# Graph attention and a two-expert layer on one core: a longer lead of blocks, routing and tables in parts, and a new order of products at each tile's start

## The chip, the cores and the metric

The kernel runs on one core of one Trainium2 chip, in one launch. The metric is the device time of that core in microseconds (us). Below, TensorE is the matmul engine, VectorE, ScalarE, GpSimd and SyncE the four others; SyncE issues most transfers.

## The reference, cut to what matters

Everything is float32. N = 4096 nodes, D = 512, E = 8 experts.

```python
q = layernorm(x) @ Wq.T + bq;  k = key @ Wk.T + bk;  v = value @ Wv.T + bv
s = (q @ k.T) / 4096 ** 0.5 * adj
s = where(abs(s) < 1e-5, -1e9, s)
x1 = x + (softmax(s) @ v) @ Wm.T + bm
g = softmax(layernorm(x1) @ Wg + bg);  the two largest of 8, renormalised to sum 1
out = x1 + sum over the two chosen e of gate_e * (layernorm(x1) @ We[e].T + be[e])
```

## The kernel before, in words

Each float32 operand is held as a high and a low half in float16, and a product is three float16 matmuls (high by high, high by low, low by high). A group of products over the 512 of the contraction, 12 matmuls of 128x512, is called a block of TensorE work here.

The first stage folds the weights (Wq with Wk, Wv with Wm), projects the values and writes the queries of all 32 tiles of 128 rows to DRAM. The keys stay in `kT`, the values in `v`.

The second stage, `attend(t)`, runs over the tiles t. A tile's 4096 scores are 8 pieces c of 512 columns. `scores(t, c)` is a block into one of four PSUM banks; VectorE adds a bias and multiplies by the adjacency (`times_adj`), ScalarE takes the absolute value (`absolute`), VectorE masks and takes the maximum (`mask`). When all 8 pieces are there, ScalarE takes exponentials (`exponent`, two passes a piece), VectorE makes the low half (`low_half`), and SyncE has the piece transposed by a DMA. `times_values(t, c)` is again a block; all 8 of a tile add up in one PSUM bank, `o_bank`. Because the exponentials need the whole row, the value products of tile t-1 are spread over the iteration of tile t, and those of its pieces 6 and 7 fall into the iteration of tile t+1. There `residual(t-2)` on VectorE reads `o_bank` (x1_done) before `times_values(t-1, 0)` may write it.

Every engine follows an order that is written out by hand, and all are in order. On VectorE the order at a tile's start is: low halves 0 to 2 of the old tile, `times_adj` 0, low half 3, `mask` 0, `times_adj` 1, low half 4, `mask` 1, low halves 5 and 6, `times_adj` 2, low half 7, `mask` 2, `residual(t-2)`. On ScalarE it is: exponents 0 to 3, `absolute` 0, exponent 4, `absolute` 1, exponents 5, 6 and 7, `absolute` 2. The queries of the next tile are fetched from DRAM when the last scores of this one are done.

After each tile the rows are routed: layer norm, `gate_logits` on TensorE, `route_top2` and `route_gates` on VectorE, `ranks` on TensorE, `route_slots` on VectorE; GpSimd then scatters the normed rows to slots in DRAM, region by region for each expert (`scatter_row`). The tokens are in two halves, each with its own table of 39 blocks of 128 slots. `tables(h)` on VectorE computes it in 19 dependent steps: after tile 17 for half 0, within the last stage for half 1.

The third stage runs 78 blocks: SyncE loads the block's 128 rows, TensorE turns them (`turn_block`) and multiplies with the expert's weights (`multiply_block`), VectorE adds the bias (`block_bias`), ScalarE multiplies with the gate (`block_gate`), GpSimd adds the rows to the output in DRAM by an indirect DMA (`add_block`). An add waits for the four-back one, and at the first block of an expert's run for the ones before it in its half. The first LEAD blocks are all of half 0, the last LEAD of half 1, and the middle ones alternate between the halves. The experts' weights, split into halves during the second stage and kept in DRAM, are loaded over `kT` by `load_expert` on ScalarE's queue.

Of the kernel before, what the change touches and what calls it, by code (L numbers as in the profile page):

```python
# [19 lines left out]
def graph_attention_moe_kernel(nc, x, adj, keyT, valueT, Wq, bq, Wk, bk, Wv, bv, WmT, bm, Wg, bg, WeT, be, outs):  # L20
# [37 lines left out]
    LEAD = 15  # L58
# [22 lines left out]
    with ctx:  # L81
# [173 lines left out]
        we_dram = nc.dram_tensor("we_halves", (2 * E, P, 2, 2 * D), F16, kind="Internal").ap()  # L255
# [154 lines left out]
        def _(sp):  # L410
# [101 lines left out]
            def pad_first_regions():  # L512

                sp.wait_ge(tables_done, 1)
                for e in range(E):
                    at = sp.value_load(pad_at[0:1, 0, e:e + 1], min_val=0, max_val=(DUMMY - 1) * P)
                    sp.dma_start(slots[0][bass.ds(at, P), :], pad_row[:, :]).then_inc(padded[0], 16)
# [9 lines left out]
            pad_first_regions()  # L527
# [43 lines left out]
            expert_ready(1)  # L571
            turn_rows(T - 1)
            expert_ready(2)
            for st in lead[9:]:
                load_block(st)
            for e in range(3, E):
                expert_ready(e)
            sp.wait_ge(slotted, 32 * T)
# [12 lines left out]
        def _(pool):  # L591
# [92 lines left out]
            scatter_row(T - 2, 1, 0)  # L684
            for st in lead_steps():
                add_block(st)
                if st.first == 0:
                    scatter_row(T - 2, 1, 1)
                if st.first in (6, 8):
                    scatter_row(T - 1, 1, int(st.first == 8))  # L690
# [11 lines left out]
        def _(act):  # L702
# [12 lines left out]
            def project(g, last=False):  # L715
# [15 lines left out]
                for j in range(KC):  # L731
                    if j == (0 if last else 1):
                        act.wait_ge(key_loaded, g * 16 + 16)
                        nc.scalar.activation(kT[:, 0, :, bass.ds(g * GW, GW)], key_in, ACT.Copy).then_inc(key_hi, 1)
# [45 lines left out]
            def store_piece(i, q):  # L780
# [3 lines left out]
                nc.scalar.dma_start(we_dram[i, :, :, q * WP:(q + 1) * WP], we_halves).then_inc(piece_stored, 16)  # L784
# [17 lines left out]
            def attend(t, routes, splits=False, stores=False):  # L802

                last = isl(t, T)
                exponent(t - 1, 0)
# [4 lines left out]
                for c in range(1, 4):  # L810
                    exponent(t - 1, c)
# [32 lines left out]
                if routes:  # L844
# [25 lines left out]
            for c in range(C):  # L870
                exponent(T - 1, c)
                if c == 1:
                    load_expert(3)
            act.wait_ge(p_hi, T * C)
# [4 lines left out]
            gap_exponent(T - 2)  # L879
# [21 lines left out]
            for st in lead:  # L901
# [25 lines left out]
        def _(dve):  # L927
# [58 lines left out]
            def project(g, last=False):  # L986
# [26 lines left out]
                for j in range(KC):  # L1013
# [7 lines left out]
                    if j == (0 if last else 1):  # L1021
                        dve.wait_ge(key_hi, g + 1)
                        nc.vector.tensor_tensor(kT[:, 1, :, bass.ds(g * GW, GW)], key_in,
                                                kT[:, 0, :, bass.ds(g * GW, GW)], ALU.subtract).then_inc(key_lo, 1)
# [149 lines left out]
            def tables(h):  # L1174

                n = [0]

                def step(ins):
# [438 lines left out]
```

## Time and profile before

| | |
|---|---|
| median of 3 runs (lowest, highest) | 1893.38 us (1889.34, 1895.35) |
| profiled execution, its own time | 1882.06 us |
| its span, first to last instruction | 1880.0 us |
| instructions in it | 33385 |
| TensorE busy | 1814.6 us, 97% of the span |
| VectorE, ScalarE, GpSimd busy | 1182.7, 737.8, 254.8 us |
| mean granted TensorE clock | 0.988 of full speed |

The shares of busy time are means over stages with different limits. TensorE's busy time is made from modelled ends that overlap by 0.16 us between matmuls, so what counts is the stretches in which it stood idle, and which wait ended them.

### The profile page before, as it was taken

The numbers are of one execution on the slowest core, as the hardware profiler recorded it, in microseconds if no ns is written. First come the engines' busy times: TensorE is split into PE (matmuls) and PEld (weight loads), VectorE is DVE, ScalarE is ACT, GpSimd is POOL, SyncE is SP. The second block draws the span as 40 slices with busy tenths as digits, with TensorE's granted clock in tenths as the row PEclk, the third lists the DMA queues.
The fourth block names the chain that finished last, engine by engine and source line by source line (L and its number), as shares of the span: only waits on it lengthen the run. The fifth ranks groups of instructions, "written<-read, shape, count | busy, mean of one in ns | idle before, by whom it ended". The sixth has DMA issues, their size and how long they took to land.

```text
span 1880.0 us, 33385 instructions
## 1 busy us (share of the span) xinstructions
PE 1814.6 (97%) x8730; PEld 849.4 (45%) x8731; DVE 1182.7 (63%) x3116; ACT 737.8 (39%) x1429; POOL 254.8 (14%) x277
## 2 busy tenths in 40 slices
PE   8999999999999999999999999999999998779997
PEld 4544444444444444444444444444444444335553
DVE  2888766666666666666666666666666664534543
ACT  1444444444344334444433333334443333223333
POOL 1000000010000000111000000001110000335544
PEclk9999999999999999999999999999999999989999
DMA  6355556666676666666656655555655669889986
GB/s 202 113 179 190 171 139 145 158 161 162 158 168 160 163 154 156 162 163 163 157 135 172 147 133 140 133 129 134 143 142 133 143 151 217 215 211 202 171 148 85
DMA packets 442717, 296.47 MB, mean 158 GB/s; under 512 B 319025, under 2 KB 351793, under 8 KB 442674
## 3 DMA queue, kind: packets, MB, share of 16 engines
q1 hardware_dynamic: 388562, 228.25, 49.1%
q0 software_dynamic: 16736, 38.35, 11.1%
q10 hardware_dynamic: 37376, 29.38, 5.7%
q8 instruction: 17, 0.28, 0.1%
q14 instruction: 26, 0.21, 0.0%
HBM read 152.68 MB, written 67.72 MB: 117 GB/s over the span
## 4 chain that ended last, share of the span: by engine, by line
PE 72%; DVE 8%; DMA 8%; issue 5%; ACT 2%; ACTq 2%; SPq 2%; DVEq 1%; POOLq 0%; POOL 0%
PE ps L1370 15%; PE ps L1372 15%; PE ps L1371 15%; PE ps L1473 8%; PE ps L1475 8%; PE ps L1474 8%; DMA work<-q_scratch 4%; DVE work L1046 2%; PE ps L1379 2%; DMA out<-val_region,tok_ids 1%; ACT work L752 1%; PE ps L1544 1%; DVE work L1330 1%; DVE work L1053 1%; PE ps L1417 1%
## 5 line engine op out<-in xcount | busy, mean ns | idle before, releaser
L1370 PE MATMUL ps<-key_region,work 128*128 128x512 f16 (+1 forms) x1336 | 509.8, 382 | 16.2 <-DMA work<-q_scratch 14.5
L1371 PE MATMUL ps<-key_region,work 128*128 128x512 f16 (+1 forms) x1336 | 509.3, 381 | 0.0
L1372 PE MATMUL ps<-key_region,work 128*128 128x512 f16 (+1 forms) x1336 | 508.8, 381 | 0.0
L1473 PE MATMUL ps<-val_region,work 128*128 128x512 f16 x1024 | 388.8, 380 | 6.1 <-DVE work L1088 6.0
L1475 PE MATMUL ps<-val_region,work 128*128 128x512 f16 x1024 | 389.0, 380 | 0.0
L1474 PE MATMUL ps<-val_region,work 128*128 128x512 f16 x1024 | 389.0, 380 | 0.0
L752 ACT ACTIVATE work<-work 128x512 f32<-128x512 f32 x256 | 161.3, 630 | 568.2 <-DVE work L1046 567.8
L1046 DVE SCALAR_TENSOR_TENSOR work<-ps,r_cur,work 128x512 f32<-128x512 f32 x256 | 191.7, 749 | 164.1 <-PE ps L1372 149.1
L1068 DVE TENSOR_TENSOR work<-work 128x512 f16<-128x512 f32 x256 | 176.2, 689 | 83.8 <-ACT work L765 83.3
L1370 PEld LDWEIGHTS ps<-key_region,work 128*128 128x128 f16 x1336 | 131.2, 98 | 179.3 <-issue 35.1
L760 ACT ACTIVATE work<-work,exp_bias 128x512 f32<-128x512 f32 x256 | 181.6, 710 | 70.7 <-DVE exp_bias L1064 54.6
L1056 DVE CUSTOM_DVE_ANT_0 work<-work 128x512 f32<-128x512 f32 x256 | 177.3, 692 | 49.4 <-DVE work L1053 49.4
L1372 PEld LDWEIGHTS ps<-key_region,work 128*128 128x128 f16 x1336 | 131.3, 98 | 158.9 <-issue 3.2
L1371 PEld LDWEIGHTS ps<-key_region,work 128*128 128x128 f16 x1336 | 131.2, 98 | 147.8 <-issue 3.0
L765 ACT ACTIVATE work<-work,exp_bias 128x512 f16<-128x512 f32 x256 | 180.7, 706 | 0.0
L1053 DVE TENSOR_SCALAR work<-work 128x512 f32<-128x512 f32 x256 | 109.2, 427 | 112.0 <-ACT work L752 107.8
L1475 PEld LDWEIGHTS ps<-val_region,work 128*128 128x128 f16 x1024 | 100.3, 98 | 121.6 <-issue 1.1
L1473 PEld LDWEIGHTS ps<-val_region,work 128*128 128x128 f16 x1024 | 100.1, 98 | 121.1 <-issue 7.5
L1474 PEld LDWEIGHTS ps<-val_region,work 128*128 128x128 f16 x1024 | 100.2, 98 | 113.8 <-issue 0.8
L675 POOL DMA_INDIRECT out<-val_region,tok_ids x78 | 121.4, 1556 | 126.9 <-DMA out<-val_region,tok_ids 73.0
L641 POOL COPY work<-gate 128x1 f32<-128x1 f32 x62 | 21.0, 339 | 861.5 <-DVE slots_u L1172 764.2
L1322 DVE TENSOR_TENSOR work<-ps,work 128x512 f16<-128x512 f32 x78 | 53.9, 691 | 104.1 <-ACT work L886 104.0
(161 smaller groups left out, 1574.8 us busy)
## 6 DMA issues: line engine op xcount, KB each, us to landing
work<-in_adj SPq DMA_DIRECT2D x256, 256.0 KB, 2.9
val_region<-slots SPq DMA_DIRECT2D x58, 257.0 KB, 4.6
work<-in_valueT SPq DMA_DIRECT2D x8, 1024.0 KB, 6.7
work<-in_x SPq DMA_DIRECT2D x8, 1024.0 KB, 5.2
work<-in_keyT SPq DMA_DIRECT2D x8, 1024.0 KB, 5.5
q_scratch<-work SPq DMA_DIRECT2D x8, 1024.0 KB, 5.1
work<-q_scratch SPq DMA_DIRECT2D x32, 256.0 KB, 3.0
work<-in_x SPq DMA_DIRECT2D x32, 256.0 KB, 3.0
```

Of the source, the lines that this page charges most:

```text
L752: nc.scalar.activation(w[:, c * CW:(c + 1) * CW], s_adj[:, c % 2, :], ACT.Abs).then_inc(abs_done, 1)
L760: nc.scalar.activation(prob[:, c % 2, :], w[:, c * CW:(c + 1) * CW], ACT.Exp, bias=exp_bias[:, :], scale=1.0 / SS, accum_out=sum_part[:, c ...
L765: nc.scalar.activation(p_split[:, c, 0:CW], w[:, c * CW:(c + 1) * CW], ACT.Exp, bias=exp_bias[:, :], scale=1.0 / SS).then_inc(p_hi, 1)
L1046: nc.vector.scalar_tensor_tensor(s_adj[:, c % 2, :], s_bank(c), r_cur[:, :], adj_in[:, c % ADJ, :], ALU.add, ALU.mult).then_inc(s_read, 1)
L1056: nc.vector.tensor_tensor_reduce(out=masked, in0=s_adj[:, c % 2, :], in1=masked, scale=1.0, scalar=-3.0e38, op0=ALU.add, op1=ALU.max, accu ...
L1068: nc.vector.tensor_tensor(p_split[:, c, CW:2 * CW], prob[:, c % 2, :], p_split[:, c, 0:CW], ALU.subtract).then_inc(p_lo, 1)
L1370: nc.tensor.matmul(bank, st[0], mv[0], start=(k == 0), stop=False)
L1371: nc.tensor.matmul(bank, st[0], mv[1], start=False, stop=False)
L1372: last = nc.tensor.matmul(bank, st[1], mv[0], start=False, stop=(k == n - 1))
L1473: nc.tensor.matmul(bank, st[0], mv[0], start=first, stop=False)
L1474: nc.tensor.matmul(bank, st[0], mv[1], start=False, stop=False)
L1475: last = nc.tensor.matmul(bank, st[1], mv[0], start=False, stop=final)
```

## The change

- LEAD goes from 15 to 23, so 23 blocks of half 0 stand first, 32 alternate, and 23 of half 1 stand last.
- At each tile's start TensorE's order changes from scores 0, scores 1, values 6, scores 2, values 7, scores 3 to values 6, scores 0, values 7, scores 1, scores 2, scores 3 (values are those of tile t-2, pieces 6 and 7). The order on VectorE and ScalarE around it stays, but for ScalarE's store and load of a weight piece, which move from after exponent 0 to after exponent 3.
- `tables(h)` becomes four functions, `count_blocks`, `sum_blocks`, `spread_blocks`, `mark_blocks`, put between pieces of tile 18 for half 0 and after blocks 9, 10, 11 and 12 for half 1.
- The routing steps of the last three tiles are put later, and one by one between blocks. The writes of the pad rows of half 1 go from ScalarE (after block 9) to SyncE.
- The split weights lie in DRAM and in SBUF so that an expert's half is one run of 4 KB in each partition instead of four of 1 KB; the keys' layout follows. Experts 5, 6 and 7 are loaded after blocks 1, 3 and 5 instead of 0, 1 and 2.

```diff
-    LEAD = 15
+    LEAD = 23
...
-        kT = key_region[:, :].rearrange("p (h k n) -> p h k n", h=2, k=KC)
+        kT = key_region[:, :].rearrange("p (c h k n) -> p c h k n", c=C, h=2, k=KC)
...
-        we = key_region[:, :].rearrange("p (a h k e o) -> p e a h k o", h=2, e=E, a=2, k=KC // 2)
+        we = key_region[:, :].rearrange("p (e k c h w) -> p e k h c w", e=E, k=KC, c=2, h=2)
+        we_parts = key_region[:, :].rearrange("p (i f) -> p i f", i=2 * E)
...
             def attend(t, routes):          # TensorE
-                scores(t, 0)
-                scores(t, 1)
+                for c in range(LAG):
+                    if routes:
+                        times_values(t - 2, C + c - LAG)
+                    scores(t, c)
                 for c in range(C):
                     if c >= LAG:
                         times_values(t - 1, c - LAG)
-                    elif routes:
-                        times_values(t - 2, C + c - LAG)
...
             def load_expert(e):             # ScalarE's queue
                 for a in range(2):
-                    nc.scalar.dma_start(we[:, e, a].rearrange("p h k o -> p (h k) o"),
-                                        we_dram[2 * e + a].rearrange("p h (k o) -> p (h k) o", o=D)).then_inc(we_loaded[e], 16)
+                    nc.scalar.dma_start(we_parts[:, 2 * e + a], we_dram[2 * e + a]).then_inc(we_loaded[e], 16)
...
-                if st.first + 5 < E:
-                    load_expert(st.first + 5)
-                if st.first + 3 < E:
-                    load_bias(st.first + 3)
-                if st.first == 4:
+                if st.first in (1, 3, 5):
+                    load_expert((st.first + 1) // 2 + 4)
+                if st.first in (0, 1, 2, 4, 6):
+                    load_bias(3 + (st.first if st.first < 2 else st.first // 2 + 1))
+                if st.first == 1:
+                    gap_exponent(T - 2)
+                if st.first == 6:
                     gap_exponent(T - 1)
-                if st.first == 9:
-                    act.wait_ge(tables_done, 2)
-                    for e in range(E):
-                        at = act.value_load(pad_at[0:1, 1, e:e + 1], min_val=0, max_val=(DUMMY - 1) * P)
-                        nc.scalar.dma_start(slots[1][bass.ds(at, P), :], pad_row[:, :]).then_inc(padded[1], 16)
...
-            dve.wait_ge(piece_stored, 16 * PIECES * 2 * E)      # VectorE
-            tables(0)
-            first_slots(1)
-            with dve.Fori(TH + 2, T) as t:
+            attend(TH + 2, 1, counts=True)
+            with dve.Fori(TH + 3, T - 1) as t:
                 attend(t, 1)
+            attend(T - 1, 1)
...
+                if st.first == 1:
+                    route_top2(T - 2)
+                if st.first == 2:
+                    route_gates(T - 2)
                 if st.first == 4:
-                    route_top2(T - 1)
-                    route_gates(T - 1)
-                if st.first == 1:
                     route_slots(T - 2)
                 if st.first == 6:
+                    route_top2(T - 1)
+                if st.first == 7:
+                    route_gates(T - 1)
+                if st.first == 9:
                     route_slots(T - 1)
-                    tables(1)
+                    count_blocks(1)
+                if st.first == 10:
+                    sum_blocks(1)
+                if st.first == 11:
+                    spread_blocks(1)
+                if st.first == 12:
+                    mark_blocks(1)
...
             lead = lead_steps()             # TensorE
             for c in range(C):
                 times_values(T - 1, c)
-                if c == 5:
-                    gate_logits(T - 2)
...
                 if st.first == 0:
+                    gate_logits(T - 2)
+                if st.first == 3:
                     ranks(T - 2)
-                if st.first == 3:
+                if st.first == 5:
                     gate_logits(T - 1)
-                if st.first == 5:
+                if st.first == 8:
                     ranks(T - 1)
```

## Rows read from the trace of the kernel before

**Rows 1.** Stretches: length, busy PE, PEld, DVE, ACT, POOL, granted clock, DMA share, GB/s.

```profile
240.00:1550.00 1310.00, 1289.30 (x6196) 582.83 (x6195) 859.04 (x2348) 535.03 (x1118) 109.32 (x146) 1.00 0.63 150
1550.00:1676.00 126.00, 99.06 (x468) 46.88 (x467) 57.07 (x198) 32.91 (x62) 27.99 (x27) 0.91 0.86 211
1676.00:1868.00 192.00, 191.59 (x1009) 103.16 (x1006) 94.13 (x248) 75.78 (x126) 98.36 (x64) 1.00 0.89 164
```

**Rows 2.** TensorE's waits over the span: us in total, times, longest.

```profile
PE ps L1370 <- DMA work<-q_scratch: 14.5, 27, 0.9
PE ps L1544 <- DVE work L1322: 11.4, 3, 8.1
...
PE ps L1473 <- DVE work L1088: 6.0, 1, 6.0
...
PE ps L1490 <- DVE picked L1160: 2.9, 1, 2.9
```

**Rows 3.** TensorE in order of time around one tile's start: start, duration.

```profile
1187.73 0.39 PE L1370 MATMUL ps<-key_region,work 128*128 128x512 f16 x1 [0.43 <-DMA work<-q_scratch]
...
1192.92 0.38 PE L1473 MATMUL ps<-val_region,work 128*128 128x512 f16 x1
...
1203.28 0.38 PE L1473 MATMUL ps<-val_region,work 128*128 128x512 f16 x1
```

**Rows 4.** ScalarE in order of time at the same tile's start.

```profile
1194.83 0.63 ACT L752 ACTIVATE work<-work 128x512 f32<-128x512 f32 x1 [0.81 <-DVE work L1046]
1195.36 0.71 ACT L760 ACTIVATE work<-work,exp_bias 128x512 f32<-128x512 f32 x1
...
1196.07 0.70 ACT L765 ACTIVATE work<-work,exp_bias 128x512 f16<-128x512 f32 x1
1196.68 0.70 ACT L760 ACTIVATE work<-work,exp_bias 128x512 f32<-128x512 f32 x1
...
1199.59 0.63 ACT L752 ACTIVATE work<-work 128x512 f32<-128x512 f32 x1 [0.18 <-DVE work L1046]
```

**Rows 5.** VectorE in order of time at the same tile's start.

```profile
1193.96 0.75 DVE L1046 SCALAR_TENSOR_TENSOR work<-ps,r_cur,work 128x512 f32<-128x512 f32 x1
...
1198.12 0.69 DVE L1068 TENSOR_TENSOR work<-work 128x512 f16<-128x512 f32 x1 [0.62 <-ACT work L765]
1198.73 0.75 DVE L1046 SCALAR_TENSOR_TENSOR work<-ps,r_cur,work 128x512 f32<-128x512 f32 x1
...
1200.87 0.69 DVE L1056 CUSTOM_DVE_ANT_0 work<-work 128x512 f32<-128x512 f32 x1 [0.19 <-DVE work L1053]
...
1201.49 0.75 DVE L1088 SCALAR_TENSOR_TENSOR work<-ps,inv_sum,work 128x512 f32<-128x512 f32 x1
```

**Rows 6.** VectorE and TensorE at tile 18's `residual`.

```profile
988.20 0.75 DVE L1088 SCALAR_TENSOR_TENSOR work<-ps,inv_sum,work 128x512 f32<-128x512 f32 x1
...
989.09 0.59 PE L1473 MATMUL ps<-val_region,work 128*128 128x512 f16 x1 [5.97 <-DVE work L1088]
```

**Rows 7.** Short stretches around idle gaps of TensorE, with the columns of rows 1.

```profile
987.60:994.40 6.80, 5.31 (x13) 1.95 (x14) 4.72 (x11) 1.26 (x2) 0.57 (x1) 0.50 0.76 186
1626.00:1633.00 7.00, 3.77 (x21) 1.77 (x20) 4.82 (x21) 2.40 (x5) 1.14 (x1) 1.00 0.82 260
1640.36:1646.40 6.04, 3.35 (x10) 1.68 (x11) 4.40 (x19) 1.21 (x2) 4.60 (x5) 0.72 1.01 128
1615.70:1622.50 6.80, 5.81 (x23) 2.65 (x24) 0.00 (x0) 0.47 (x1) 1.18 (x2) 0.50 1.07 341
1656.70:1666.90 10.20, 4.84 (x14) 2.18 (x15) 3.01 (x8) 2.61 (x5) 2.18 (x2) 0.50 0.76 187
1670.30:1673.70 3.40, 3.34 (x8) 1.27 (x9) 0.69 (x1) 0.40 (x1) 0.00 (x0) 0.50 1.06 286
```

**Rows 8.** Issues on ScalarE's queue in the third stage.

```profile
1613.51 5.31 ACTq L796 DMA_DIRECT2D key_region<-we_halves  x2
...
1650.23 10.25 ACTq L916 DMA_DIRECT2D slots<-pad_row  x8
```

More of the change, by code:

```diff
@@ L571, in _ @@
             expert_ready(1)
+            for st in lead[9:13]:
+                load_block(st)
+            sp.wait_ge(gate_mm, T - 1)
             turn_rows(T - 1)
             expert_ready(2)
-            for st in lead[9:]:
+            for st in lead[13:TOKS]:
                 load_block(st)
-            for e in range(3, E):
+            expert_ready(3)
+            expert_ready(4)
+            for st in lead[TOKS:]:
+                load_block(st)
+            for e in range(5, E):
                 expert_ready(e)
+            pad_regions(1)
             sp.wait_ge(slotted, 32 * T)
@@ L804, in attend @@
                 last = isl(t, T)
-                exponent(t - 1, 0)
+                for c in range(4):
+                    exponent(t - 1, c)
                 if stores:
@@ L809, in attend @@
                     load_piece(t - 2, 0)
-                for c in range(1, 4):
-                    exponent(t - 1, c)
                 absolute(t, 0)
@@ L843, in attend @@
                     load_expert(2)
-                if routes:
+                if routes and not last:
                     gap_exponent(t - 2)
@@ L1236, in piece_low, with attend @@
                                                ALU.mult, ALU.subtract).then_inc(piece_lo, 1)
-            def attend(t, h=None):
+            def attend(t, h=None, counts=False):
                 splits = h == 0
+                last = isl(t, T)
                 for c in range(3):
@@ L1262, in attend @@
                 mask(t, 3)
+                if counts:
+                    count_blocks(0)
                 if h is not None:
@@ L1271, in attend @@
                     piece_low(t - 2, 1)
+                if counts:
+                    dve.wait_ge(piece_stored, 16 * PIECES * 2 * E)
+                    sum_blocks(0)
                 times_adj(t, 5)
                 mask(t, 5)
+                if counts:
+                    spread_blocks(0)
                 times_adj(t, 6)
@@ L1277, in attend @@
                     piece_low(t - 2, 2)
-                if h is not None:
+                if counts:
+                    mark_blocks(0)
+                    first_slots(1)
+                if h is not None and not last:
                     route_top2(t - 2)
@@ L1285, in attend @@
                     piece_low(t - 2, 3)
-                if h is not None:
+                if h is not None and not last:
                     route_slots(t - 2)
@@ L1520, in attend_last @@
                 t = T - 1
-                scores(t, 0)
-                scores(t, 1)
-                for c in range(C - LAG, C):
-                    times_values(t - 2, c)
+                for c in range(LAG):
+                    times_values(t - 2, C + c - LAG)
+                    scores(t, c)
                 for c in range(2, 6):
@@ L1529, in attend_last @@
                 times_values(t - 1, 1)
-                gate_logits(t - 2)
                 scores(t, 7)
@@ L1533, in attend_last @@
                     times_values(t - 1, c)
-                    if c == 4:
+                    if c == 3:
+                        gate_logits(t - 2)
+                    if c == 6:
                         ranks(t - 2)
@@ L1555, in multiply_block @@
                 product(y_bank(st.bank), [((tokT[:, st.bank, 0, k, :], tokT[:, st.bank, 1, k, :]),
-                                         (we[:, e, k // 2, 0, k % 2, :], we[:, e, k // 2, 1, k % 2, :])) for k in range(KC)]).then_inc(y_mm, 1)
+                                         (we[:, e, k, 0], we[:, e, k, 1])) for k in range(KC)]).then_inc(y_mm, 1)
             lead = lead_steps()
```

61 lines of the change are left out of this document (33 added, 28 removed).

## The prediction

> **What bounds the kernel now.** I read the page first: TensorE is busy 97% of the span and no other engine over 63%, so only what TensorE does, and where it stands idle, counts. The view by stretches [rows 1] shows where that is. In the second stage, from 240 to 1550 us, it is idle 1310.0 - 1289.3 = 20.7 us. In the stretch where routing, the last tile's values and the first blocks meet, from 1550 to 1676 us, it is idle 126.0 - 99.1 = 26.9 us of 126, at a mean clock of 0.91. From 1676 to 1868 us, all blocks, it never stops. The view of waits [rows 2] names the ends of that idle time: 27 short waits at a tile's start for the queries' transfer (14.5 us), one of 6.0 us for `residual` (L1088) after `tables(0)`, and in the last stage 11.4 us for VectorE's token halves (L1322), which were late because of the tables and of ScalarE's queue. So there are two sums: the tile's start, which is paid 29 times (tiles 2 to 30; tile 1 has no old values, and the last tile has an order of its own), and the joint between the stages, which is paid once.
>
> **The new order at a tile's start.** What it removes is plain. The queries' wait goes, since values 6 now stands ahead of scores 0 and gives the transfer one block more: two scores blocks start at 1187.73 and the next block at 1192.92 [rows 3], so a block is 2.59 us, and the longest of these waits is 0.9 [rows 2]. A wait costs 0.16 us more than its idle time, because the listed matmul of 0.38 us overlaps the next by that much (2.59 / 12 = 0.22 between starts). That gives back 14.5 + 27 x 0.16 = 18.8 us.
>
> What it adds is a wait that isn't there today. `times_values(t-1, 0)` may not overwrite `o_bank` before `residual(t-2)` has read it, and on VectorE that stands behind `mask` 2, which stands behind a chain that begins with scores 1. Today scores 1 is TensorE's second block of the tile and four blocks follow before values 0: hand-over at 1192.92, values 0 at 1203.28 [rows 3]. After the change scores 1 is the fourth block, and only scores 2 and 3 lie behind it, 5.18 us. I count from the moment at which scores 1 hands over TensorE:
> - `times_adj` 1 can start when the last matmul has ended, 0.16 later; I take 0.20.
> - `absolute` 1 starts 0.87 after it (1193.96 [rows 5] to 1194.83 [rows 4]): 1.07. ScalarE has this ahead of exponents 5, 6 and 7, so these wait too. They did their first four long before.
> - Exponent 5 starts 0.53 later, 1.60. A pair of passes takes 1195.36 to 1196.68 = 1.32, so exponent 6 starts at 2.92, its second pass 0.71 later at 3.63, and ends at 4.33 (0.70 long) [rows 4].
> - Low half 6 follows within 0.03, at 4.36. VectorE has it ahead of `times_adj` 2, which starts 0.61 later (1198.12 to 1198.73), at 4.97, though scores 2 is long done.
> - `absolute` 2 is 0.86 after it (1198.73 [rows 5] to 1199.59 [rows 4]), 5.83; exponent 7 is over by then (4.24 + 1.32 = 5.56). The second pass of the mask starts 1.28 after `absolute` 2 (1199.59 to 1200.87), 7.11, and `residual` 0.62 later, 7.73 [rows 4, 5].
> - values 0 started 0.89 after the start of a late `residual` (988.20 to 989.09) [rows 6]: 8.62.
>
> Values 0 so starts 8.62 - 5.18 = 3.44 us late. Today it has room: `residual` starts at 1201.49, plus 0.89 is 1202.38, and values 0 starts at 1203.28, 0.9 us later [rows 3, 5]. Nothing makes good for it later, since every engine's work of the next tile hangs on TensorE's scores; so each of 29 tiles grows by 3.44: 99.8 us. In the first 16 of them ScalarE also issues a weight piece's store and load ahead of `absolute` 0. Moved behind exponent 3 these lie in ScalarE's wait for scores 0 and cost nothing; they are not in the chain above, which starts later.
>
> **Tables in parts, half 0.** The 6.0 us wait goes: no part stands ahead of `residual`. It cost 6.0 + 0.16, and behind it the clock stood at 0.50 for 6.8 us with 5.3 us of TensorE work in it [rows 7], so half of that, 2.7. Back: 8.8 us. The parts themselves fall between pieces, where the four score banks cover some 2 us each.
>
> **The clock.** An idle gap of 3.3 us (3.44 less the 0.16) comes 29 times. What the rows show of such gaps: the granted clock fell at the end of the 2.7 us gap from 1640.36 (3.35 us of work at 0.50: the mean of that stretch is 0.72), and it fell after the ones of 6.0 and 8.1 us; but over the gap of 2.9 us, the wait for `picked` between 1626 and 1633, it stayed at 1.00 [rows 2, 7]. So a gap of 3.3 us is of a size at which it may fall or not. I take every second one, at the price of the shortest fall: 3.35 / 2 = 1.7 us. 29 x 0.5 x 1.7 = 24.7 us; the bounds are 0 and 49.3. The Trainium skill (TensorE: Matmul & The Clock Gate, section on why this matters for your kernels) tells the author to avoid idle gaps of about this size between bursts of matmuls, since the clock goes back to its lower level. By that rule all would fall, and the sum would be 24.6 us higher. The trace agrees in three of the gaps named and not in the one of 2.9 us.
>
> **The joint between the stages.** All that can be had is the 26.9 us of idle time [rows 1] and what the low clock cost: 5.8 + 3.35 + 4.8 + 3.3 = 17.3 us of work at 0.50 [rows 7], half of it 8.7; together 35.6. Most causes are taken up: the 8.1 us wait stood behind ScalarE's eight pad writes (10.25 us of its queue [rows 8]), which go to SyncE; the wait from 1640.4 stood behind the lump of `tables(1)`; the weight loads that held ScalarE's queue 5.3 us [rows 8] have a quarter of the runs and come every second block. `gate_logits` and `ranks` come two or three blocks later than their inputs need. What is late next is half 1: its tables are ready after block 12, SyncE then writes the pads (about 10 us by the rate on ScalarE), they must land, and then block 23 is loaded; at 3.0 us a block (192 us [rows 1] hold 63 blocks and some) that is close to block 21, where it is needed. And less stall is more transfers in less time: the DMA share is already 0.86 in that stretch, and 0.89 after it [rows 1], in which adds and loads ran at TensorE's pace. So I don't take all: three quarters, 26 us, between bounds of 0 and 35.6.
>
> **Layouts, order of adds.** The keys' new layout is the same 512 columns in a row to the matmul. An expert's weights are now read as two runs of 256 columns. No row shows that for a matmul. Below is nothing; above, the nearest row is the matmul that starts anew after a wait, 0.39 us against 0.38 [rows 3], and if the second run cost as much, 936 x 0.01 = 9.4 us. I take nothing: from 1676 to 1868 us the expert's weights for one contraction already lie in parts, and TensorE loses nothing there [rows 1]. 23 blocks of one half at the end instead of 15 wait more often for their predecessors' adds; but GpSimd caught up within each run, and the last 12 us after TensorE stay.
>
> **Sum.** 99.8 + 24.7 - 18.8 - 8.8 - 26 = +70.9 us. Against the profiled execution of 1882.1 that is 1953.0. That one is 11.3 us below the median of the runs, 1893.4, and the forecast goes by the median: 1893.4 + 70.9 = 1964.3.
>
> **Rivals.**
> - The gaps don't lower the clock: 99.8 - 18.8 - 8.8 - 26 = +46.2, 1939.6. For it: the 2.9 us gap. Against: the 2.7 us one.
> - Every gap does: +95.5, 1988.9. This is where the skill's rule leads too.
> - The joint gains nothing, because transfers bind there: +96.9, 1990.3. For it: the DMA share; against: most of that idle time ended on VectorE and ScalarE, not on a transfer.
> - Faster: `residual` comes in time after all, by VectorE reaching `mask` 2 before values 0 is due, so that the order only removes waits. Then -18.8 - 8.8 - 26 = -53.6, 1839.8. It decides where the new wait is under 53.6 / 29 = 1.85 us a tile, that is if the chain from scores 1 to values 0 took under 7.0 us instead of 8.6. Against: each link is an in-order engine's next instruction, with today's durations.
>
> **Chances and range.** The forecast 0.50, with a range of its own of 1950 to 1980; clock stays 0.20; clock always falls 0.14; joint without gain 0.10; faster 0.06. Range 1928 to 2000: from the first rival with a joint that gives all 35.6 (1930.0) to the two upper ones with room to the next. About 0.3% is what a measurement of this kernel can tell from no change. Faster by more than that 0.06, within it 0.01, slower 0.93.
>
> **What the profile after would show.** In the waits, L1473 for VectorE's L1088 some 29 times with about 3.3 us each, and no wait for the queries. A tile of about 45 us instead of 42. In ScalarE's order `absolute` 1 with idle time before it and exponents 5 to 7 behind. Mean clock a little down, with falls spread over the second stage. In the joint under 10 us of idle time. I would be wrong if L1088 shows no wait, or if its wait is short because a link above is skipped.

## The result, and the profile after

The changed kernel takes 2001.5 us in the median (1997.2 to 2005.2, 4 runs), the kernel before 1891.4 on the same chip: a ratio of 1.0595, with a 95% interval of 1.0556 to 1.0635. It is slower by 110 us, in the direction that was forecast, and lies 1.5 us above the top of the range (2000). The forecast was 1964.3, so 37 us are missing.

TensorE's longest waits in the changed kernel (us in total, times, longest one):

```profile
PE ps L1506 <- DVE work L1094: 94.7, 29, 3.3
PE ps L1523 <- DVE picked L1166: 17.1, 2, 16.0
PE ps L1516 <- DMA work<-work: 13.8, 2, 9.7
PE ps L1506 <- DMA work<-work: 10.3, 2, 6.0
```

The first line answers to the third of [rows 2]: `times_values` (now L1506) waits for `residual` (now L1094) not once but 29 times, 3.3 us each. The waits for the queries are gone. The other three lines lie in the last tiles and the first blocks. In the third, TensorE waits at `gate_logits` for the turned rows, and in the fourth at `times_values` for the turned probabilities; both are transposes by DMA. The kernel before had such a wait too, which stands in no row ahead of the prediction:

```profile
PE ps L1483 <- DMA work<-work: 9.0, 3, 4.7
```

So the waits for transposes went from 9.0 us to 13.8 + 10.3 = 24.1 us.

The stretches, with the columns of rows 1, cut at the moment at which TensorE starts the value products of tile 29, at 1597.6 us (1498.6 before):

```profile
240.00:1598.00 1358.00, 1263.28 (x5951) 566.33 (x5950) 829.93 (x2262) 513.71 (x1081) 86.61 (x140) 0.98 0.57 139
1598.00:1714.00 116.00, 100.64 (x439) 43.18 (x437) 51.09 (x145) 32.21 (x66) 6.51 (x11) 0.91 0.83 153
1714.00:1786.00 72.00, 43.20 (x227) 22.70 (x228) 27.73 (x107) 15.16 (x27) 18.48 (x15) 0.81 0.76 190
1786.00:1991.00 205.00, 202.74 (x1055) 108.14 (x1053) 102.33 (x280) 79.64 (x132) 103.28 (x70) 1.00 0.84 168
```

And the kernel before, from the same moment to its first block, and from there to where its stalls end:

```profile
1499.00:1595.00 96.00, 91.58 (x447) 41.32 (x446) 52.12 (x153) 32.20 (x67) 8.03 (x11) 1.00 0.80 183
1595.00:1676.00 81.00, 58.44 (x267) 28.61 (x265) 35.59 (x130) 19.12 (x32) 24.25 (x22) 0.85 0.83 206
```

The profiled executions lie further apart than the medians: the one of before (1882.1 us) is below all its four runs (1886.2 to 1895.4), and the changed one (2005.2) is the longest of its four. The moment of the cut splits the difference of their spans, 2003.5 - 1880.0 = 123.5 us: 1597.6 - 1498.6 = 99.0 us came up to it, in 29 tiles, and 24.5 us after it, in what the prediction called the joint. In the joint the last tiles, up to the moment at which TensorE starts to turn the first block, took 116 us instead of 96, with 15.4 us idle and a clock of 0.91 instead of 4.4 and 1.00. The first blocks stalled for 28.8 us instead of 22.6, but from the turning of block 0 to that of block 23 both kernels took the same time, 100.2 and 100.7 us. After that TensorE was almost fully busy again, as before [rows 1].

One tile of the changed kernel, VectorE in order of time, to be laid beside [rows 5]:

```profile
1176.31 0.75 DVE L1052 SCALAR_TENSOR_TENSOR work<-ps,r_cur,work 128x512 f32<-128x512 f32 x1 [2.21 <-PE ps L1405]
...
1180.47 0.69 DVE L1074 TENSOR_TENSOR work<-work 128x512 f16<-128x512 f32 x1 [0.62 <-ACT work L774]
1181.08 0.75 DVE L1052 SCALAR_TENSOR_TENSOR work<-ps,r_cur,work 128x512 f32<-128x512 f32 x1
...
1183.22 0.69 DVE L1062 CUSTOM_DVE_ANT_0 work<-work 128x512 f32<-128x512 f32 x1 [0.19 <-DVE work L1059]
...
1183.83 0.75 DVE L1094 SCALAR_TENSOR_TENSOR work<-ps,inv_sum,work 128x512 f32<-128x512 f32 x1
```

and ScalarE and TensorE in the same tile:

```profile
1177.17 0.63 ACT L761 ACTIVATE work<-work 128x512 f32<-128x512 f32 x1 [3.11 <-DVE work L1052]
...
1184.73 0.38 PE L1506 MATMUL ps<-val_region,work 128*128 128x512 f16 x1 [3.28 <-DVE work L1094]
```

VectorE waits 2.2 us for scores 1 and ScalarE 3.1 us for VectorE, with exponents 5 to 7 behind it. From `times_adj` 1 to values 0 it takes 1184.73 - 1176.31 = 8.42 us; the prediction had 8.62 - 0.20 = 8.42. VectorE and ScalarE run the same instructions in the same order as before, and the rows of before give the same length: 1201.49 + 0.89 - 1193.96 = 8.42 [rows 5, 6].

In the joint, first a stretch of GpSimd and then two waits of VectorE. L654 scatters the routed rows, L685 adds a block to the output:

```profile
1736.87 1.56 POOL L685 DMA_INDIRECT out<-val_region,tok_ids  x1 [9.00 <-DMA out<-val_region,tok_ids]
1754.08 1.55 POOL L685 DMA_INDIRECT out<-val_region,tok_ids  x1 [15.65 <-DMA out<-val_region,tok_ids]
...
1767.19 1.02 POOL L654 DMA_INDIRECT slots<-work,slots_u  x1 [0.84 <-POOL work L651]
```

```profile
1700.02 0.55 DVE L1117 TENSOR_SCALAR work<-work,moments,rstd 128x512 f32<-128x512 f32 x1 [11.47 <-DMA slots<-work,slots_u]
...
1774.86 0.15 DVE L1160 TENSOR_SCALAR den<-egap 128x1 f32<-128x1 f32 x1 [16.25 <-DMA slots<-work,slots_u]
```

The slots of tile 30 were there at 1738.2 us, but its scatter stands behind adds 0 to 4, which wait for each other, and was issued at 1767. `route_gates` of tile 31 (L1160) waits for it, since the scatter reads the gates, and VectorE's work for two blocks waits behind that: the 16.0 us of TensorE. The same pair one tile earlier (L1117, `route_rows` of tile 30, behind the scatter of tile 29) held VectorE 11.5 us.

The last tiles lose their time elsewhere. Once the rows of tile 29 are turned, SyncE issues seven transposes of probabilities in a row. This is the first of them, changed and before, and then the 20 us from there on (columns of rows 1):

```profile
1654.21 6.95 SPq L483 DMA_TRANSPOSE work<-work  x1
1654.20:1674.20 20.00, 12.32 (x56) 4.95 (x54) 10.22 (x31) 8.97 (x20) 0.00 (x0) 0.90 1.20 152
```

```profile
1553.71 1.23 SPq L481 DMA_TRANSPOSE work<-work  x1
1553.70:1573.70 20.00, 17.61 (x91) 8.18 (x92) 11.31 (x38) 9.16 (x22) 1.73 (x2) 1.00 0.82 203
```

In the changed kernel the first three took 7.0, 5.8 and 6.6 us to issue, where a transpose of the second stage takes 1.2 us in the median; the seven came to 25.9 us instead of 9.2. Their queue moved 0.70 MB in these 20 us instead of 1.68, while the DMA engines were busier (a share of 1.20 instead of 0.82; a packet counts whole where it starts, so this can pass 1) and moved fewer bytes in all (152 instead of 203 GB/s). ScalarE's queue with the weight loads moved 2.32 MB instead of 2.11.

### The profile page after: what moved, and what is told of

It is laid out like the page before. It is cut to its first block, busy times and chain, and to the rows that moved or that the text cites. A ratio compares the mean times of both kernels' runs of the same rounds, so it can differ in the third digit from the quotient of the medians.

```text
span 2003.5 us, 33154 instructions
## 1 busy us (share of the span) xinstructions
PE 1844.6 (92%) x8730; PEld 856.9 (43%) x8731; DVE 1183.9 (59%) x3116; ACT 734.8 (37%) x1429; POOL 234.5 (12%) x277
## 4 chain that ended last, share of the span: by engine, by line
PE 79%; DMA 6%; ACT 5%; DVE 4%; issue 4%; SPq 1%; DVEq 0%; POOLq 0%; ACTq 0%; POOL 0%
PE ps L1403 14%; PE ps L1404 14%; PE ps L1405 14%; PE ps L1506 11%; PE ps L1508 11%; PE ps L1507 11%; DMA out<-val_region,tok_ids 3%; DVE work L1052 2%; ACT work L769 2%; ACT work L774 2%; PE ps L1412 1%; PE ps L1577 1%; ACT work L761 1%; DMA work<-work 1%; DVE work L1094 1%
## 5 line engine op out<-in xcount | busy, mean ns | idle before, releaser
L1506 PE MATMUL ps<-val_region,work 128*128 128x512 f16 x1024 | 401.0, 392 | 105.1 <-DVE work L1094 94.7
L1507 PE MATMUL ps<-val_region,work 128*128 128x512 f16 x1024 | 402.0, 393 | 0.0
L1508 PE MATMUL ps<-val_region,work 128*128 128x512 f16 x1024 | 401.8, 392 | 0.0
L1506 PEld LDWEIGHTS ps<-val_region,work 128*128 128x128 f16 x1024 | 102.0, 100 | 236.6 <-issue 119.2
L1508 PEld LDWEIGHTS ps<-val_region,work 128*128 128x128 f16 x1024 | 102.9, 100 | 129.4 <-issue 14.9
L1507 PEld LDWEIGHTS ps<-val_region,work 128*128 128x128 f16 x1024 | 102.3, 100 | 116.6 <-issue 11.6
L685 POOL DMA_INDIRECT out<-val_region,tok_ids x78 | 120.8, 1549 | 145.3 <-DMA out<-val_region,tok_ids 68.7
L902 ACT ACTIVATE val_region<-work,tok_gates 128x512 f32<-128x512 f32 x78 | 56.3, 722 | 167.4 <-DVE work L1352 167.4
L651 POOL COPY work<-gate 128x1 f32<-128x1 f32 x62 | 12.8, 207 | 874.4 <-DVE slots_u L1178 781.1
```

The lines of the kernel that those rows point to most:

```text
L1506: nc.tensor.matmul(bank, st[0], mv[0], start=first, stop=False)
L1507: nc.tensor.matmul(bank, st[0], mv[1], start=False, stop=False)
L1508: last = nc.tensor.matmul(bank, st[1], mv[0], start=False, stop=final)
```

## The experiments

Each ratio is to the kernel before on the same chip. Some differences between two other kernels are between chips, on which the kernel before had medians of 1887.9 to 1894.6 us. "Joint" is the time from the start of tile 29's value products to the end of the profiled span: 381.4 us before, 405.9 us changed.

### TensorE's order alone

The kernel before with this edit and nothing else (the second half is the last tile, which lies in the joint):

```diff
-                scores(t, 0)
-                scores(t, 1)
+                for c in range(LAG):
+                    if routes:
+                        times_values(t - 2, C + c - LAG)
+                    scores(t, c)
                 for c in range(C):
                     if c >= LAG:
                         times_values(t - 1, c - LAG)
-                    elif routes:
-                        times_values(t - 2, C + c - LAG)
...
-                scores(t, 0)
-                scores(t, 1)
-                for c in range(C - LAG, C):
-                    times_values(t - 2, c)
+                for c in range(LAG):
+                    times_values(t - 2, C + c - LAG)
+                    scores(t, c)
```

> The kernel before with nothing changed but TensorE's order at a tile's start. If the wait for the residual is the whole price of the new order: 29 waits on VectorE's residual of about 3.3 us, about 15 falls of the clock, no waits for the queries, so 99 + 30 - 19, about 105 to 115 us over the kernel before (near 2000 us), and the joint between the stages as it was. If instead the other parts (layout, tables, routing) made the second stage slower, it stays under +60 us.

1998.2 us, ratio 1.0569 (1.0531 to 1.0607): +103.6 us. 29 waits for `residual`, 98.3 us, one of them 6.7 where `tables(0)` stands; joint 392.9. So the order alone is nearly the whole result. The joint grows by 11.5 us, though nothing in it is edited but the start of the last tile.

### The old order in the changed kernel

The reverse edit, in the changed kernel.

> The changed kernel with the old order of TensorE put back, all else as changed. By the theory of two separate prices the second stage falls back to about 42.3 us a tile and what is left is the joint, dearer by about 24 us, less 9 us for the tables in parts: about 10 to 20 us over the kernel before. The rival, that the joint is only bad because TensorE comes to it late or cold, gives the forecast's gain: 20 to 35 us under the kernel before.

1884.3 us, ratio 0.9955 (0.9921 to 0.9989), joint 385.8. The expectation of 10 to 20 us over the kernel before was wrong, and so was the rival's 20 to 35 under it: it is 10 us under. Everything else in the change is worth that little, and what is gained lies in the second stage: the two tile distances around the tables of half 0 are 86.1 us together instead of 93.2. The joint is 4 us dearer, not 26 cheaper. The wait for `picked` (17.4 us) is there in this kernel too.

### The residual early

The changed kernel, with this on VectorE:

```diff
                 mask(t, 1)
+                if h is not None:
+                    residual(t - 2)
                 low_half(t - 1, 5)
...
                 mask(t, 2)
                 if h is not None:
-                    residual(t - 2)
                     route_stats(t - 2)
```

> The changed kernel with VectorE's residual moved ahead of low half 5, right behind mask 1; TensorE's order as changed. If the chain from scores 1 through exponents 5 to 7 and mask 2 is the price, residual starts about 3.0 us after the hand-over of scores 1, values 0 finds it done 1.3 us before it is due, no wait and no fall of the clock is left in the second stage, and a tile takes 41.7 us: 125 to 135 us under the changed kernel, about 1870. If something else holds values 0 (its turned probabilities, say), a wait of about 3 us stays with another releaser.

1859.3 us, ratio 0.9827 (0.9795 to 0.9859): 142 us under the changed kernel. Between 240 and 1500 us TensorE has a single wait left, 1.1 us for `picked`.

A tile takes 41.69 us instead of 45.12 (without a fall of the clock), so the wait cost 3.43 us a tile. The clock does not fall in the second stage. The joint is 384.5 here, 21 us less than in the changed kernel, though neither the routing nor the runs in it were touched. This is why the gain is above the 125 to 135 expected.

### The residual in the middle

The same move, but only ahead of `mask` 2.

> The changed kernel with the residual between low half 7 and mask 2, which by the chain starts it at 6.3 us and values 0 at 7.2, so 2.0 us late instead of 3.4. The wait falls to 1.9 us, 29 times. If a gap of that size never lowers the clock, the gain is 29 x 1.4 + 30 = 70 us; if the clock falls as often as with 3.3 us, it is 41 us.

1930.8 us, 70.7 under the changed kernel, against 70 expected for gaps that leave the clock alone. TensorE waits for `residual` 29 times, 1.8 us each, 53.1 us in all. A tile takes 43.69 us, 28 times alike. So 29 gaps of 1.8 us brought no fall of the clock, and up to this earlier point, too, the chain has the length that was read for it. The joint is 399.0 us, 7 less than in the changed kernel.

### The scatter ahead of the adds, and tile 29's routing back

Both on the kernel with the residual early. The first:

```diff
+            scatter_row(T - 2, 1, 0)
             for st in lead_steps():
                 add_block(st)
-                if st.first in (4, 5):
-                    scatter_row(T - 2, 1, int(st.first == 5))
+                if st.first == 0:
+                    scatter_row(T - 2, 1, 1)
```

> The kernel with the residual early (1859 us), with one more edit: GpSimd scatters tile 30's rows ahead of the first add and behind it, as in the kernel before, instead of behind adds 4 and 5. Theory: the 16 us wait for picked comes because route_gates of tile 31 on VectorE waits for that scatter, which stands behind adds that wait for each other. The scatter then starts with tile 30's slots, after block 4, and its two landings take some 12 us, so the wait falls to 3 to 8 us: 8 to 15 us faster, about 1848. Rival, that transfers are simply slow there: no change.

The mechanism was right: the wait for `picked` fell from 16.4 to 3.3 us. The time did not follow: 1858.0 us against 1859.3. TensorE then waited 3.4 us at block 23 for half 1's rows, the link that the prediction had named as next, 4.0 us at block 36, and took 3.4 to 3.5 us instead of 3.03 for blocks 62 to 66. Up to the turning of block 23 this kernel is 12 us ahead of the one with the residual early, and after it 12 us slower.

The second puts `route_top2`, `route_gates`, `route_slots`, `gate_logits` and `ranks` of tile 29 back into the iteration of tile 31.

> The kernel with the residual early, with the routing of tile 29 put back into the iteration of tile 31, as in the kernel before; the rest of the joint as changed. Theory: the waits of TensorE for the last tile's turned probabilities (6.7 us) come because its low halves stand behind route_slots of tile 29 and behind route_rows of tile 30, which waits for tile 29's scatter. They go: 6 to 10 us faster, and the 16 us wait for picked stays. Rival: the low halves were late anyway, no change.

1860.5 us (1855.1 to 1864.8), no change, though the routing itself no longer stood ahead of the low halves. A wait of 6.0 us for turned probabilities stayed. This theory of that wait fell.

### LEAD alone

The kernel before with LEAD 23.

> The kernel before with LEAD 23 and nothing else. By the forecast's reading the 1.7 us wait for half 1's rows and part of the stall behind the pad writes can be hidden only if half 1 starts later, so 2 to 5 us faster at most, since VectorE's tables and ScalarE's pad writes still stop the blocks. Rival: 46 of 78 blocks without alternation make the adds the bound, and it is 5 us or more slower.

1883.7 us, ratio 0.9978 (0.9953 to 1.0003): within the measurement. The wait for half 1's rows is gone, the other stalls of the joint stay.

### The joint's routing as before

The residual early, the first scatter edit, tile 29's routing back, and tiles 30 and 31 routed and scattered where the kernel before had them. LEAD 23, the tables in parts (after blocks 6 to 9), the pads on SyncE and the long runs stay.

```diff
             for c in range(C):
                 times_values(T - 1, c)
+                if c == 5:
+                    gate_logits(T - 2)
...
                 if st.first == 0:
-                    gate_logits(T - 2)
-                if st.first == 3:
                     ranks(T - 2)
-                if st.first == 5:
+                if st.first == 3:
                     gate_logits(T - 1)
-                if st.first == 8:
+                if st.first == 5:
                     ranks(T - 1)
```

> The residual early, LEAD 23, tables in parts (after blocks 6 to 9), pad writes on SyncE and weights in longer runs as changed, but routing and scatters of tiles 29, 30 and 31 where the kernel before had them. Theory: what was wrong in the changed joint is the order of routing alone, and the parts that remain take away the pad, table and weight stalls: some 15 to 25 us under the kernel with the residual early, about 1838. Rival, that LEAD or the transfers cost as much as they save: 1850 to 1860.

1847.6 us, ratio 0.9779 (0.9733 to 0.9826), joint 375.8: 12 us under the kernel with the residual early (9 by the ratios and by the joints), less than the 15 to 25 expected, and the fastest kernel of the study that computes the whole result, 2.2% under the kernel before.

### Short runs again

The weights' and keys' layout of the kernel before, once in that fastest kernel and once in the changed one. The loads of an expert, out of an edit that changes the layouts with them:

```diff
-                    nc.scalar.dma_start(we_parts[:, 2 * e + a], we_dram[2 * e + a]).then_inc(we_loaded[e], 16)
+                    nc.scalar.dma_start(we[:, e, a].rearrange("p h k o -> p (h k) o"),
+                                        we_dram[2 * e + a].rearrange("p h (k o) -> p (h k) o", o=D)).then_inc(we_loaded[e], 16)
```

> The kernel with the joint's routing as before (1847.6 us), with the weights' and keys' layout put back, so four runs of 1 KB a partition instead of one of 4 KB. There TensorE waited 7.3 us for the last tile's turned probabilities, four transposes took 17 us to issue instead of 11, and two weight loads landed after 13.4 us instead of 8.6. Theory: the long runs crowd out the transposes' short packets, so the wait goes and it is 6 to 10 us faster, about 1839. Rival: the transposes are late for another reason, the sum of traffic, and the short runs cost ScalarE's queue what they cost before: no change or 3 us slower.

1853.8 us (1853.0 to 1854.4), 6 us slower. The two were measured on different chips; against the kernel before on its own chip the ratio is 0.9800 instead of 0.9779, which would be 4 us. In the profiles 4 us lie before the value products of tile 29 (the residual of tile 28 starts at 1473.6 us instead of 1469.4), where `ranks` now waits for `picked` in some tiles; the joint is 1 us longer. So the long runs pay there by some 4 to 6 us, and the theory that they crowd out the transposes fails in this kernel.

> The changed kernel with the weights' and keys' layout alone put back. By the same theory the waits for turned probabilities (10.3 us) and the scatter of tile 29 that took 10 us to land shrink: 8 to 15 us under the changed kernel's 2001.5. By the rival, that these waits come from the order of routing, under 3 us.

1980.5 us (1973.2 to 1995.6), 21 us under the changed kernel, with a joint of 377.7 instead of 405.9. The waits for turned probabilities fell from 10.3 to 4.9 us, those for turned rows from 13.8 to 1.4, while the one for `picked` stays (15.7). So that wait and a joint shorter than that of the kernel before (381.4) stand together in one kernel.

### LEAD 15 in the fastest kernel

> The kernel with the joint's routing as before (1847.6 us), with LEAD 15 again. Half 1's tables are ready after block 9, the pads and the first rows need some 17 us more, which is block 15, and block 15 is turned at 13: a wait of 5 to 8 us there that LEAD 23 hides. Theory: 4 to 8 us slower, about 1853. Rival: what the later half gives back is taken by adds that wait more often, so no change.

1861.5 us (1855.7 to 1867.3), 14 us slower, with one wait of 15.9 us for half 1's first rows, at least twice as long as expected. In the profiled pair the difference is 7.8 us, all of it in the joint. So LEAD 23 is worth something once tables and pads are later than before, and nothing alone.

### The kernel before with two orders

TensorE's new order and the early residual, nothing else.

> The kernel before with two edits only: TensorE's new order and VectorE's residual right behind mask 1. Second stage at 41.7 us a tile: 19 us for the queries' waits and a part of the 9 us at the tables; the joint as before. 19 to 26 us under the kernel before, about 1868. If the joint grows as it did under the new order alone (12 us more), about 1880.

1874.5 us (1867.2 to 1881.8), ratio 0.9925 (0.9893 to 0.9956), between the two expected values. A tile takes 41.7 us in most of the second stage, one wait of 3.6 us for `residual` is left at `tables(0)`, and the joint is 391.7, again 10 us longer than before with nothing edited in it but the last tile's start.

### Routing back, and both back, in the changed kernel

> The changed kernel with routing and scatters of tiles 29, 30 and 31 where the kernel before had them, the tables of half 1 after blocks 6 to 9, all else as changed: TensorE's new order and the long runs stay. If the order of routing is the dear part of the changed joint, the 16 us wait for picked and the waits for turned probabilities shrink and it is 20 to 30 us under the changed kernel's 2001.5. If the long runs are, the waits for turned probabilities stay and it is 8 to 12 us under it, as the same edit gave with the residual early.

> The same with the weights' and keys' layout put back too. If the two prices add, 21 us (the layout alone) and 10 to 12 us: near 1970. If they are one price, the same transfers arriving late in the same places, it is no better than the better of the two alone, near 1980.

1978.4 us (1973.5 to 1986.1) with the routing back, 1979.6 (1971.3 to 1989.4) with both, where the layout alone gave 1980.5. The joints are 377.2, 377.8 and 377.7. Either edit takes 28 us off the joint in the profiles (21 to 23 us off the medians), and the second nothing more. The prices don't add; that it is one and the same price is not shown, since they come off in different places (table below). The second stage of the profiled kernel with both back is 12 us longer than the changed kernel's, with 18 falls of the clock in 28 tiles instead of 14.

### Writes in place of adds

The kernel with the scatter first (1858.0 us), its adds to the output made into plain writes:

```diff
-                    in_=y_out[:, st.b8, :], in_offset=None, compute_op=ALU.add)
+                    in_=y_out[:, st.b8, :], in_offset=None)
```

> The kernel with the residual early and the scatter first (1858.0 us), with the last rows written to the output instead of added to it; this leaves out the sum of the residual rows and of the two experts. The 13 us taken off the wait for picked there gave nothing, since blocks 23, 36 and 60 to 66 came late instead. If those are late because adds, which read and write, are paced by the transfers, they are on time now, and it is 8 to 14 us faster, about 1847. If they are late through VectorE's and ScalarE's own order, no change.

1840.2 us: 18 us faster, more than expected. (Without the adds this kernel leaves out the sums with the residual rows and of the two experts.) The stretch from 1660 to 1800 us, with adds and with writes (columns of rows 1):

```profile
1660.00:1800.00 140.00, 133.73 (x677) 70.83 (x678) 61.91 (x166) 50.02 (x83) 70.69 (x47) 0.96 0.91 189
```

```profile
1660.00:1800.00 140.00, 140.00 (x743) 76.17 (x742) 69.28 (x185) 55.45 (x92) 46.10 (x48) 1.00 0.59 184
```

The DMA share falls from 0.91 to 0.59 and TensorE is never idle in that stretch: no block after the twelfth is late. So the adds' transfers took what the shorter wait for `picked` had given. The Trainium skill (DMA: Bandwidth & Descriptors, rules for kernel authors) says that an accumulating DMA reads its destination and writes it later; the fall of the share is in line with that.

## Why the prediction was right about the tile and wrong about the joint

**The queries' wait.** Right: no such wait is left in the changed kernel.

**The chain from scores 1 to values 0.** Right: 8.42 us from `times_adj` 1 to values 0, read and measured; 3.44 us a tile forecast, 45.12 - 41.69 = 3.43 measured; with the residual ahead of `mask` 2, the same links give 2.0 us late, and it was 43.69 - 41.69 = 2.00. That nothing else holds values 0 is shown by the early residual, which takes the wait away.

**Tables in parts, half 0.** Right in what mattered: no wait of 6 us is left at tile 18. The 8.8 us were not measured alone; the two tiles around the tables are 93.2 - 86.1 = 7.1 us shorter with the parts, at TensorE's old order.

**Layouts.** Right: blocks 62 to 77 take 45.4 us in the kernel before and in the one with the residual early, which has the new layout.

**The clock.** The forecast was every second gap, 24.7 us. The distances of 28 successive residuals in the changed kernel are 45.1 us 14 times, 46.8 ten times and 47.9 four times, so the clock fell in 14 of 28 tiles, at 1.7 or 2.8 us: 10 x 1.7 + 4 x 2.8 = 28.2 us. The term was 3.5 us short, because four falls were longer than the shortest, which was taken as the price: the granted clock was low for 3.4 us in ten of them and for 6.8 us in four. That it was every second one is a choice that came true and no derivation: three other kernels with the same gaps of 3.3 us (short runs, routing back, both back) had 13, 14 and 18 of 28. By the rule of the Trainium skill (TensorE: Matmul & The Clock Gate, section on why this matters for your kernels) each such gap would have brought one; the traces show about half. Up to tile 29 the forecast sum is 99.8 + 24.7 - 18.8 - 8.8 = +96.9, and the profiles give +99.0.

**The joint.** This is the step that failed, in sign: "three quarters, 26 us" were to come back, and 24.5 us more were spent. Those are 50.5 of the 52.6 us by which the profiled pair missed the forecast's +70.9. The time from the start of tile 29's value products to the turning of block 0, from there to the turning of block 23, and from there to the end of the span, with the time that the seven transposes took to issue, in us:

| kernel | to block 0 | to block 23 | to the end | transposes |
|---|---|---|---|---|
| before | 96.5 | 100.7 | 184.2 | 9.2 |
| changed | 116.7 | 100.2 | 188.9 | 25.9 |
| changed, old order | 98.8 | 102.6 | 184.4 | 9.5 |
| changed, residual early | 101.5 | 99.0 | 184.0 | 9.3 |
| changed, residual in the middle | 110.8 | 103.6 | 184.6 | 24.2 |
| changed, short runs | 98.6 | 94.0 | 185.2 | 12.8 |
| changed, routing back | 107.1 | 79.8 | 190.3 | 10.8 |
| changed, both back | 104.1 | 80.5 | 193.1 | 11.7 |
| residual early, scatter first | 100.1 | 88.8 | 195.8 | 9.2 |
| the same, writes for adds | 101.1 | 80.8 | 181.9 | 9.5 |

*Why the gain did not come.* "`gate_logits` and `ranks` come two or three blocks later than their inputs need" looked at TensorE's order alone. It left out the queue of GpSimd, past which the scatters of tiles 29 and 30 were moved: the scatter behind adds 0 to 4 came 29 us after its slots were ready, and VectorE waited 16 us for it with the blocks' work behind. The stalls that the change took away were replaced by this one, so that block 23 came no sooner after block 0 (100.2 us against 100.7). Nor would the 26 us have come with the scatter alone in its old place: there the adds' transfers bind, as the last two rows of the table show.

*Where the loss came from.* Not from that wait, which stays at 15.7 to 17.4 us in kernels whose joint takes 378 to 386 us. 20.2 of the 24.4 us lie ahead of the turning of block 0: 15.7 us idle instead of 4.4, at two waits for turned probabilities and one for turned rows, and 20.5 us at the low clock instead of none. The prediction put the growth of these waits at nothing: its list of causes does not name the 9.0 us that they cost before, and it gave them no bound upward. The seven transposes took over 24 us to issue in two kernels alone, and 9 to 13 in all others: the two are those with the changed routing, the long runs and a residual still behind low half 7 together; they are also the two with the longest way to block 0. "The weight loads have a quarter of the runs" was booked as a gain only; in the changed kernel short runs take 28 us off the joint.

What exactly these three do to each other is not settled. Short runs take 18 us off ahead of block 0 and 6 between blocks 0 and 23, the routing put back 10 and 20 (and gives 1 back after it), and the residual early 15 and 1. In the fastest kernel a 7.3 us wait for turned probabilities stands beside long runs and 3.5 beside short ones, at nearly the same length of the joint. The same page of the Trainium skill (section on queues, rings and completion order) says that a DMA engine takes a whole packet from one queue before it turns to the next. From that one can argue that long runs hold up the transposes everywhere; here the changed kernel's waits agree, and the fastest kernel's time does not.

The rival of the joint bound by transfers, which had 0.10, is real once the stalls are gone: with writes in place of adds 8.0 us come off between blocks 0 and 23, and 13.9 after.

**The range.** Its upper end, 2000, came from one rival at a time: every fall of the clock, or a joint without gain. The joint's gain had zero as its lower bound, and no row stood for that, though steps had been moved past other waits in it.

**Left open.** The new order lengthens the joint by 10 to 12 us in the kernel before, with the waits for the residual or without them; 6 to 8 us of it lie ahead of block 0. In the version without, TensorE waits 14.1 us in all for turned rows, where it waited 9.0 before; no run takes that apart. What makes the stretch from block 23 to the end up to 9 us longer in the kernels with the routing back is open as well; the adds' transfers are likely, but not shown there.

## What to carry to other kernels

Moving a producer later in one engine's queue is paid at the first consumer that cannot be skipped: follow the written order of the other engines from that point to the instruction that frees the buffer, with the trace's own starts, and compare with the work left in front of it. Here that gave 3.44 us against 3.43 measured, and one moved line (the residual) turned 110 us of loss into 35 of gain. A step moved past a queue of transfers that wait for each other must be priced there too. A wait that ends on a transfer belongs in the list even if the change does not touch it: in a stretch as full of transfers as this one (a share of 0.83 to 0.86 before), moved work can lengthen it, so the stretch needs a bound for loss as well as for gain. And the longest wait of a stretch need not be the reason why one kernel is slower than another there: compare the times between the same two events in both.

## What the runs showed of the hardware that was not expected

Gaps of the same 3.3 us lowered TensorE's clock in 14 of 28 tiles, in other kernels in 13 to 18, and gaps of 1.8 us in none of 29. The low clock lasted 3.4 or 6.8 us and made the tile 1.7 or 2.8 us longer.

The same transpose, 1.2 us to issue in the median, took 7.0, 5.8 and 6.6 us three times in a row, while the DMA share stood at 1.20 with only 152 GB/s moved.

Writing the blocks' rows instead of adding them, at about the same bytes per second over the stretch (184 against 189 GB/s), lowered the DMA share from 0.91 to 0.59.
